# A four-layer graph network on one core: block transposes on VectorE with a scratch round trip in place of TensorE transposes, and rows spread by DMA

## The reference, cut to what matters

```
layer 0:  e = leaky((x W1)(x W2)^T), masked by adj, softmax over rows, times (x W3), relu
layer 1:  h = x W;  e[i,j] = leaky(s1[i] + s2[j]), masked, softmax, times h, elu
layer 2:  o1 = relu(x mlp1 + b1)
          h = o1 W_fc;  e[i,j] = leaky(f1[i] + f2[j]), no mask, softmax, times h, elu, elu, + o1
          o3 = relu(that mlp2 + b2)
          h = o3 W_hand; e[i,j] = leaky(f1[i] + f2[j]), masked, softmax, times h, elu, elu, + o3, relu
layer 3:  q, k, v; four heads of 64 channels; masked softmax of q k^T / 8, times v, times wo + bo
```

## Time and profile before

| | |
|---|---|
| median of 3 runs | 2921.91 us |
| the profiled execution | 2918.28 us |
| its span | 2916.5 us |
| mean granted TensorE clock | 0.983 of full speed |
| PE busy | 92% of the span |
| DVE, ACT, POOL busy | 78%, 69%, 53% |
| DMA queue q1, share of 16 engines | 22.7% |
| DMAs that SP issues for a graph | 13 |

### The profile page before, as it was taken

How to read it: one execution, slowest core, us unless ns; L and a number is a source line. 1 busy time by engine, 2 the same in 40 slices (tenths; PEclk the granted TensorE clock), 3 DMA queues, 4 the chain that set the end, 5 groups by cost and what they waited for, 6 DMA issues and landing times.

```text
span 2916.5 us, 61536 instructions
## 1 busy us (share of the span) xinstructions
PE 2689.4 (92%) x22472; PEld 2551.3 (87%) x22472; DVE 2278.2 (78%) x6124; ACT 1998.7 (69%) x4801; POOL 1556.0 (53%) x2119
## 2 busy tenths in 40 slices
PE   4689999999999999999999999999999999999974
PEld 4589999999999999998999998999999999998863
DVE  3257888888888888888888887888888888888874
ACT  1357777777777776777777777777777777776752
POOL 0235555555555555555556555555655555555542
PEclk9799999999999999999999999999999999999997
DMA  3001222222122122212212221221222122122222
GB/s 109 19 16 37 77 81 64 57 81 80 41 80 81 59 63 80 74 47 81 80 51 71 81 72 49 81 81 48 74 81 70 52 80 80 41 81 73 66 66 73
DMA packets 132766, 195.17 MB, mean 67 GB/s; under 512 B 14832, under 2 KB 97136, under 8 KB 132464
## 3 DMA queue, kind: packets, MB, share of 16 engines
q1 hardware_dynamic: 132464, 191.24, 22.7%
HBM read 107.30 MB, written 83.89 MB: 66 GB/s over the span
## 4 chain that ended last, share of the span: by engine, by line
PE 60%; DMA 13%; ACT 8%; SPq 8%; DVE 6%; issue 4%; POOL 1%; POOLq 0%; DVEq 0%
PE ps L224 29%; DMA p4T<-scratch 10%; PE ps L378 6%; SPq L208 6%; PE ps L240 5%; PE ps L436 4%; PE ps L337 4%; PE ps L233 3%; PE ps L338 3%; DMA scratch<-p 3%; DVE p L950 3%; PE ps L456 2%; ACT p L671 2%; PE ps L360 2%; DVE h_lo L692 1%
## 5 line engine op out<-in xcount | busy, mean ns | idle before, releaser
L1067 POOL TENSOR_TENSOR p<-p,rd 128x512 f32<-128x512 f32 x256 | 269.8, 1054 | 20.0
L671 ACT ACTIVATE p<-p,nmx 128x256 f32<-128x256 f32 x512 | 255.7, 504 | 25.4 <-DVE nmx L935 25.2
L991 POOL TENSOR_TENSOR o1Tp_lo<-o1T,o1Tp_hi 128x1024 fp32r<-128x1024 f32 x64 | 153.8, 2403 | 220.8 <-ACT o1Tp_hi L472 220.8
L1003 POOL TENSOR_SCALAR xn<-act,nmean,rstd 128x256 f32<-128x256 f32 x384 | 243.6, 643 | 18.3 <-POOL rstd L998 11.2
L456 PE MATMUL ps<-p4T,v 128*64 128x256 f32 x1024 | 144.3, 404 | 118.2 <-DMA p4T<-scratch 117.7
L995 POOL TENSOR_TENSOR vare<-mv,eps 128x2 f32<-128x2 f32 x256 | 108.0, 422 | 270.5 <-DVE mv L748 270.5
L1060 POOL TENSOR_TENSOR rd<-some,den 128x2 f32<-128x2 f32 x256 | 53.5, 209 | 354.6 <-DVE den L944 354.6
L456 PEld LDWEIGHTS ps<-p4T,v 128*64 128x64 f32 x1024 | 67.3, 140 | 178.1 <-DMA p4T<-scratch 96.5
L692 DVE TENSOR_TENSOR xnT_lo<-ps,xnT_hi 128x512 fp32r<-128x512 f32 x192 | 132.1, 688 | 114.2 <-ACT xnT_hi L472 114.2
L935 DVE CUSTOM_DVE_ANT_0 p<-ps,mask 128x256 f32<-128x256 f32 x512 | 189.9, 418 | 33.3 <-PE ps L436 33.3
L480 ACT ACTIVATE sco<-sco,nmax 128x256 f32<-128x256 f32 x384 | 191.0, 500 | 28.9 <-DVE nmax L736 28.9
(11 more groups left out here) (248 smaller groups left out, 12683.1 us busy)
## 6 DMA issues: line engine op xcount, KB each, us to landing
scratch<-p SPq DMA_DIRECT2D x128, 512.0 KB, 2.9
p4T<-scratch SPq DMA_DIRECT2D x512, 128.0 KB, 3.9
x0T<-in_xT SPq DMA_DIRECT2D x64, 256.0 KB, 4.6
x<-in_x SPq DMA_DIRECT2D x64, 256.0 KB, 3.7
out<-xn SPq DMA_DIRECT2D x64, 256.0 KB, 3.0
o1T<-in_mlp SPq DMA_DIRECT2D x1, 512.0 KB, 4.4
p<-in_mlp SPq DMA_DIRECT2D x1, 512.0 KB, 4.5
att<-in_fc SPq DMA_DIRECT2D x1, 512.0 KB, 5.4
```

The source lines that it names most:

```text
L671: ins = nc.scalar.activation(rows_, rows_, ACT.Exp, scale=-1.0, bias=nmx4[:, h, m:m + 1], accum_out=den4[:, h, m:m + 1])
L991: return G.tensor_tensor(lo, whole, hi.bitcast(fp32), ALU.subtract)
L1003: ins = G.tensor_scalar(xn[:, m, :], y[:, m, :], nmean[i][:, m:m + 1], rstd[i][:, m:m + 1], ALU.add, ALU.mult)
L1067: G.tensor_tensor(rows_, rows_, rd4[:, h, :].unsqueeze(2).unsqueeze(3).broadcast_to([P, NT, QUADS, CT * QP]), ALU.mult).then_inc(S["p4n"], 1)
```

## The change

All turning of probabilities follows the pattern of layer 3. `t0`, `t1`, `t3` on DVE turn 32 by 32 blocks of `sco` into the buffer `act`; SP writes `act` to scratch (`o0`, `o1`, `o3`) and reads it back into `sco` with four DMAs (`i0`, `i1`, `i3`); ACT copies the high part from there and POOL now makes the low part. The mixed layer's output takes the same way (`o3` on DVE through `sco[2]`, then `o5` and `i5` on SP into the new `o3r`), and `r3` adds it in two instructions. The spread of columns is done by SP: `r1`, `r2`, `r3` write 256, 512 and 256 single numbers from `cols` to scratch, `f1`, `f2`, `f3` read the row back into all 128 partitions. The sums of layer 2 are made by four matmuls of 256 columns against a full square of ones, and DVE takes the reciprocal of all 256 of them. `n4` moves to POOL. `xn3` and `sco` change in shape or number, `x0T` and `pfc` share the memory of their low parts, the banks of PSUM get other tenants, and all five tables are new.

```diff
-    "sp": "lt:0 o40:7 st:9 o42:7 lx:1 i40:7 i42:7",
-    "pe": "h3:8 a0:3 v4:9 f3:8 x0:5 g0:2 s40:9 d2:7 x1:6 t3:8 s42:9 v2:7 a3:8 m2:6 h0:2 b2:7 n2:6 o3:8 w2:7 s0:2 h1:5 c2:6 f1:5 t0:2 a4:9 r2:6 t1:5 x3:8 y4:9 m3:7 n3:7 a1:5 f2:6 q4:8 k4:8",
+    "sp": "r2:5 f2:5 st:9 o5:6 r3:6 o1:3 lx:1 f3:6 lt:0 i1:3 o3:6 o0:1 i3:6 i0:1 i5:6 o40:7 r1:2 o42:7 f1:2 i40:7 i42:7",
+    "pe": "k4:8 n2:5 d2:6 v4:8 v2:6 s40:8 w2:6 x0:3 s42:8 a1:4 h1:3 c2:5 a3:7 g0:1 r2:5 a0:2 m3:6 h0:1 x1:4 a4:8 h3:6 m2:4 s0:1 x3:7 y4:8 q4:7",
...
+            def pro_out(i):
+
+                def step(t):
+                    sp.wait_ge(S[f"pro{i}_x"], t + 1)
+                    wait(sp, S[f"pro{i}_dma"], back(t - 1))
+                    sp.dma_start(scratch_pro[i].rearrange("p w n -> p (w n)"), flat(act[i])).then_inc(S[f"pro{i}_dma"], 16)
+                return step
+
+            def pro_in(i):
+
+                def step(t):
+                    sp.wait_ge(S[f"pro{i}_dma"], sent(t))
+                    rows_ = sco[i][:, :, :, :].rearrange("p b a n -> p (b a n)").rearrange("p (q n) -> p q n", q=QUADS)
+                    for w in range(QUADS):
+                        sp.dma_start(rows_[w * QP:(w + 1) * QP, :, :], scratch_pro[i][:, w, :].rearrange("(q j) n -> j q n", q=QUADS)).then_inc(S[f"pro{i}_dma"], 16)
+                return step
...
+            def at_out(i):
+
+                def step(t):
+                    sp.wait_ge(S[f"at{i}"], t + 1)
+                    wait(sp, S[f"at{i}_dma"], back(t - 1, 1))
+                    sp.dma_start(scratch_at[i].rearrange("m p -> p m"), cols[i][:, :, 1], allow_slow_non_contiguous=True).then_inc(S[f"at{i}_dma"], 16)
+                return step
+
+            def at_in(i, tile, before):
+
+                def step(t):
+                    sp.wait_ge(S[f"at{i}_dma"], sent(t, 1))
+                    wait(sp, *before(t))
+                    sp.dma_start(tile[:, :, 0, :], scratch_at[i].unsqueeze(0).broadcast_to([P, NT, P])).then_inc(S[f"at{i}_dma"], 16)
+                return step
...
-            def t0(t):
-                pe.wait_ge(S["pro0"], t + 1)
-                transposes(bank[0], sco[0]).then_inc(S["proT0_mm"], 1)
...
-                for m in range(NT):
-                    for k in range(NT):
-                        for i in (1, 0):
-                            ins = nc.tensor.matmul(ps[:, 5, 2 * m:2 * m + 2], pfcp[i][:, k, m * P:(m + 1) * P], ones2[:, :],
-                                                   start=(k == 0 and i == 1), stop=(k == NT - 1 and i == 0))
+                for k in range(NT):
+                    for i in (1, 0):
+                        ins = nc.tensor.matmul(ps[:, 5, 0:N], ones2[:, :], pfcp[i][:, k, :], start=(k == 0 and i == 1), stop=(k == NT - 1 and i == 0))
...
             def u1(t):
-                ac.wait_ge(S["f1_mm"], t + 1)
-                graph_scores(1, 1).then_inc(S["raw1"], 1)
+                ac.wait_ge(S["at1_dma"], back(t, 1))
+                graph_scores(sco[1], 1).then_inc(S["raw1"], 1)
...
             def t0(t):
-                dv.wait_ge(S["proT0h"], t + 1)
-                low_part(proT[0], bank[0]).then_inc(S["proT0"], 1)
+                dv.wait_ge(S["pro0"], t + 1)
+                wait(dv, S["xn0"], t)
+                turn(0).then_inc(S["pro0_x"], 1)
...
             def d2(t):
                 dv.wait_ge(S["d2_mm"], t + 1)
-                V.reciprocal(rdc[:, :], ps[:, 5, 0:4:2]).then_inc(S["rdc"], 1)
+                wait(dv, S["att"], t)
+                V.reciprocal(rdb[:, :], ps[:, 5, 0:N]).then_inc(S["rdb"], 1)
...
             def r3(t):
-                dv.wait_ge(S["on3_mm"], t + 1)
+                dv.wait_ge(S["o3_dma"], back(t))
                 dv.wait_ge(S["q3"], t + 1)
-                V.tensor_tensor(act[2][:, :, :], act[2][:, :, :], bank[2], ALU.add).then_inc(S["r3"], 1)
+                for m in range(NT):
+                    row = act[2][:, m, :].rearrange("p (k q c) -> p k q c", k=CT, q=QUADS)
+                    ins = V.tensor_tensor(row, row, o3r[:, :, :, m, :].rearrange("p q k c -> p k q c"), ALU.add)
+                ins.then_inc(S["r3"], 1)
...
+            def n4(t):
+                norm(3, xn3, xn3, S["rstd3"], S["xn3"], t)
...
+            def t0(t):
+                po.wait_ge(S["proT0h"], t + 1)
+                low_of_turned(proT[0], 0).then_inc(S["proT0"], 1)
```

More of the change, by code:

```diff
@@ L163, in by_quads, with by_tiles, flat, sent @@
             return row.rearrange("p (b w j) -> p w b j", b=CT, w=QUADS)
+        def by_tiles(row):
+            return row.rearrange("p (b n) -> p b n", b=CT)
+        def flat(tile):
+            return tile[:, :, :].rearrange("p a n -> p (a n)")
+        def sent(t, n=QUADS):
+            return 16 * (n + 1) * t + 16
+        def back(t, n=QUADS):
+            return 16 * (n + 1) * (t + 1)
         def wait(eng, sem, n):
@@ new lines, in pro_in, with o3_out @@
+            def pro_in(i):
[5 more added lines that the diff above has]
+                return step
+            def o3_out(t):
+                sp.wait_ge(S["o3_x"], t + 1)
+                wait(sp, S["o3_dma"], back(t - 1))
+                sp.dma_start(scratch_o3.rearrange("p w n -> p (w n)"), sco[2][:, :, :, :].rearrange("p b a n -> p (b a n)")).then_inc(S["o3_dma"], 16)
@@ new lines, in o3_in @@
+            def o3_in(t):
+                sp.wait_ge(S["o3_dma"], sent(t))
+                wait(sp, S["r3"], t)
+                rows_ = o3r[:, :, :, :, :].rearrange("p q k a c -> p q (k a c)")
+                for w in range(QUADS):
+                    sp.dma_start(rows_[w * QP:(w + 1) * QP, :, :], scratch_o3[:, w, :].rearrange("(q j) n -> j q n", q=QUADS)).then_inc(S["o3_dma"], 16)
+            def at_out(i):
[4 more added lines that the diff above has]
+                return step
@@ L196, in turn_out, with at2_in @@
+            def at2_in(t):
+                sp.wait_ge(S["at2_dma"], sent(t, 2))
+                wait(sp, S["u"], t)
+                for c in range(2):
+                    sp.dma_start(by_tiles(row2[:, c, :]), scratch_at[2][c::2, :].unsqueeze(0).broadcast_to([P, NT, P])).then_inc(S["at2_dma"], 16)
             def turn_out(c):
@@ L198, in step @@
                     sp.wait_ge(S["p4x"], 2 * t + c + 1)
-                    wait(sp, p4Tin[c], 16 * QUADS * t)
-                    sp.dma_start(scratch[c], p4[c][:, :, :]).then_inc(p4out[c], 16)
+                    wait(sp, p4_dma[c], back(t - 1))
+                    sp.dma_start(scratch[c], p4[c][:, :, :]).then_inc(p4_dma[c], 16)
                 return step
@@ L240, in transposes @@
                         ins = nc.tensor.transpose(dst[:, b, a * P:(a + 1) * P], src[:, a, b * P:(b + 1) * P], ident[:, :])
-                return ins
-            def spread(dst, col):
-                for m in range(NT):
-                    ins = nc.tensor.transpose(dst[:, m * P:(m + 1) * P], col(m).broadcast_to([P, P]), ident[:, :])
                 return ins
@@ L375, in mlp2 @@
-            def mlp2(m):
-                for k in range(HT):
-                    for i, (a, b) in enumerate(PAIRS):
-                        ins = nc.tensor.matmul(bank[3][:, m, :], WP["mlp2"][a][:, k, m * P:(m + 1) * P], o2T[b][:, k, :],
-                                               start=(k == 0 and i == 0), stop=(k == HT - 1 and i == 2))
-                return ins
+                pe.wait_ge(S["pfcl"], t + 1)
+                enter(5, "att", t + 1)
+                product3(half_of(5), hfc, pfcp, NT, 2, off=2).then_inc(S["w2_mm"], 1)
@@ L395, in f3 @@
-            def f3(t):
-                pe.wait_ge(S["h3"], t + 1)
-                spread(ps[:, 3, 0:N], lambda m: cols[3][:, m, 1:2]).then_inc(S["f3_mm"], 1)
-            def t3(t):
-                pe.wait_ge(S["pro2"], t + 1)
-                transposes(bank[3], sco[2]).then_inc(S["proT2_mm"], 1)
+                enter(2, "h3", t + 1)
+                enter(3, "h3", t + 1)
+                product3(lambda m: ps[:, 2 + m, 0:C2], o3Tp, WP["hand"], CT, NT).then_inc(S["h3_mm"], 1)
             def a3(t):
@@ L735, in masked, with turn @@
                 for m in range(NT):
-                    ins = V.tensor_tensor_reduce(sco[i][:, m, :], whole(m), mask16[:, m, :], -1.0, BIG, ALU.add, ALU.min, nmax[i][:, m:m + 1])
+                    ins = V.tensor_tensor_reduce(sco[i][:, :, m, :], whole(m), by_tiles(mask16[:, m, :]), -1.0, BIG, ALU.add, ALU.min, nmax[i][:, m:m + 1])
                 return ins
+            def turn(i):
+                blocks = sco[i][:, :, :, :].rearrange("p b a n -> p (b a) n").rearrange("p c (w j) -> p w c j", w=QUADS)
+                return V.transpose(flat(act[i]).rearrange("p (w c j) -> p w c j", w=QUADS, j=QP), blocks)
             def stats(i, y, s_y, s_mv, t):
@@ L844, in v2 @@
                 dv.wait_ge(S["w2_mm"], t + 1)
+                dv.wait_ge(S["rdb"], t + 1)
                 wait(dv, S["o2T"], t)
```

370 lines of the change are left out of this document (209 added, 161 removed), and 6 rows, old and new, of the table ORDERS.

## The result

The changed kernel takes 4382.99 us (median of 4 runs, 4382.29 to 4389.12), the kernel before 2923.6 us on the same chip: a ratio of 1.500, 95% interval 1.497 to 1.503. The forecast was 2775 us and the range ended at 2920. It is half as slow again, far beyond even the slower rival's 3035.

A forecast was written before the change was run, and what follows sets the result against it. PE was taken to bound the kernel, busy 41.08 of each 42.64 us. PE's 37.4 plus 1.9 of chain and slower trips gave period 40.0; 52 x 40.0 plus 690 gave a 2770 span, 2775 us; range 2645 to 2920.

The forecast's parts named there:

- the slower rival: Trips r1 with f1 and r3 with f3 in SP's queue take 7.1 us each: period 45.0, 3035 us; chance 0.18.
- the second chain: From s42's end through layer 1's column trip to h3: 21.6 us, 1.9 beyond the 19.65 of PE's work there.
- the 3.9 of the nearest reads: Landing time assumed for layer 1's column write r1 and read f1; with issues, 8.66 us for the two.
- the latest landing of a load: 6.7 us, which with its issue gave 7.1 us a column trip, 2.5 more than the assumed 4.63.
- the prediction's own signs of being wrong: Landings under 3 or over 6 us, reciprocal over 1 us, no PE wait over 0.3, or PE waiting for DVE before s42.
- Hidden in sum: DMA work of 29 us in a period of 40, some 5000 packets added a graph, would not bound; bursts would meet.
- PE's work: PE's busy time a round falls from 41.08 to 37.4 us as transposes, spreads, narrow sums and some returns leave.
- DVE's work: DVE's busy time a round rises from 35.13 to 36.4 us through o3's turn, the wide reciprocal and blocked operands.
- The reciprocal of 256 columns: On DVE for layer 2, taken as 0.45 us, +0.3 over the narrow one, with +1.0 kept as the upper case.
- The penalty of 1.45 us for two operands in SBUF: DVE's b2, r3, e1, e3 lose their PSUM operand and contend with POOL: 0.36 us each, 1.45 together.
- the rival with DVE's order: DVE's order becomes the bound, 36.4 us of work plus 5.2 idle: period 41.6, 2860 us; chance 0.19.
- The forecast's own 40.0: Period: PE's 37.4 us plus 1.9 from the second chain, plus 0.3 for each of two trips under load.

The follow-up runs named there:

- By runs: Changed kernel with columns turned on DVE before going to scratch, written in pieces of 32 numbers (128 B) instead of single numbers: 2878.92 us, ratio 0.986 to before.
- the spread on PE: Changed kernel with the seven column DMAs removed and eight transposes on PE spreading the columns as before; scratch trips of probabilities stay: 2869.34 us, ratio 0.983.
- the last experiment: The mixed version with a3 and g0 exchanged in PE's order, so that a3 stands behind g0: 2801.7 us, ratio 0.961.
- the mixed version: Changed kernel with layer 2's column through scratch in 128 B pieces, those of layers 1 and 3 spread on PE: 2800.02 us, ratio 0.960 from three runs.

## Why the prediction was wrong

- **The step that failed** is the landing in the second chain: "for the landing I take the 3.9 of the nearest reads". For the reads back it was near (4.3 us for `f2`, 4.0 for `f3` in the round shown), but `r1` is a write of single numbers: 8.6 to 10.2 us from issue to landing for the three columns, and 8.7 in the median for such a write in the kernel before. The upper bound of the slower rival, "the latest landing of a load", was also a bound from another kind of DMA. The prediction said itself that no row shows a written transfer of 4 bytes; then the bound should have stayed open upwards, and the range with it. The slower rival named the right place, with a chance of 0.18; the range ended at 2920, below even that rival's 3035. Two of the prediction's own signs of being wrong came: landings over 6 us and a reciprocal over 1 us.
- **The waits were added up in the wrong place.** The second chain, and so the sum, held the way of one column, out by `r1` and back by `f1`; the slower rival named `r3` too, but added 2.5 us only twice. There are three columns, and SP's order makes a series of them: it waits for each write before it issues what stands behind. From the issue of a write to that of its read pass 8.6, 9.3 and 10.2 us in the round shown, 28.15 together. By runs it is 3.0, 2.5 and 1.6 (SP issues at 1497.06 and 1500.02, 1506.42 and 1508.92, 1513.79 and 1515.38), 7.05 together and 21.1 less. The period differs by 65.55 - 41.95 = 23.6 between the two forms. What makes the other 2.5 was not measured apart; PE's busy time, 44.63 us at a clock of 0.82 against 38.9 at 1.00, is the likely part.
- **Hidden in sum** was right for the load and useless for the time: 7110 packets a round, forecast as some 5000 more than before, and a DMA share of 0.40 (0.45 by runs). In the 6 us before the read of `r2` no engine moved anything. Bandwidth was not short there; completion was late.
- The Trainium skill, DMA: Bandwidth & Descriptors, section "Specifications", asks for transfers of at least 512 B, since smaller ones are read, modified and written. The runs agree with its direction (256 numbers of 4 B land after 8.7 us), but runs of 128 B, also under its bound, let their read go 2.5 us after the issue. No run here tests the reason that the page gives. I let the rule feed only the slower rival, at a price from loads.
- **PE's work** was put at 37.4 us. By runs it is 38.9 (1482.45 / 1600 x 41.95), and 38.85 with eight transposes back on PE. The direction held, 1.5 of the 3.7 did not come; PE's restarts after waits are in it, and how much they make was not settled.
- **DVE's work** was put at 36.4 and is 1990.13 / 54 = 36.85 after. That is luck, as two terms failed the opposite ways. The reciprocal of 256 columns takes 1.74 us, where 0.45 was taken and 1.16 was the upper bound:

```profile
L927 DVE RECIPROCAL rdb<-ps x64: 1720/1740/1757, 183.7 to 4268.8; 128x256 f32<-128x256 f32 x64
L922 DVE TENSOR_TENSOR pfcp<-pfcp,row x64: 691/693/695, 179.4 to 4252.4; 128x512 f32<-128x512 f32 x64
L1002 DVE SCALAR_TENSOR_TENSOR act<-act,xn x64: 654/676/693, 259.7 to 4332.8; 128x512 f32<-128x512 f32 x64
```

  It costs by the column: 1.74 / 256 = 6.8 ns each, against one turned element's 1.3 (0.67 / 512). The Trainium skill, VectorE: DVE Perf Modes, section "Walkthrough: the 8-slice pipeline in each mode", names it an iterative divide with a repeat count of 8; this trace agrees in kind, about five times a turn's price. The penalty of 1.45 us for two operands in SBUF came only in small part. The addition with the spread column in layer 2 (L922) takes 693 ns flat, as the form with PSUM had the earlier trace rows; `e1` and `e3` take 423 ns in the median for 128x256, where `e0`, still from PSUM, takes 418; only `r3` pays, 1.03 us on the average for its two in place of 0.69. The last line is the very operation of the earlier trace rows with the median of 1050: it takes 676 ns in the new order, with the same operands. So two SBUF operands alone don't make the penalty; what runs beside them is the likely cause, which was not tried. Other operations grew in turn: the three instructions `act<-act` from 1.82 to 2.53 us a graph.
- **What held only in looks.** By runs the period is 41.95, close to the 41.6 of the rival with DVE's order. But with the spread on PE the period was about the same (41.89), and there less work on DVE made it longer and a move in PE's order made it shorter: PE's order paced. Only the last experiment points to DVE, at 40.70. The forecast's own 40.0 lies near the mixed version's 40.66, which is another kernel; the mechanism behind 40.0 was not the one that ran.

## What to carry to other kernels

Give a DMA its price by its own kind and shape of piece; if no row shows one, say that the upper end is unknown, and turn the data so that pieces are runs (here 32 numbers, 128 B) before they leave. In one ordered queue, add up every write that is read back a place or two later, wherever the engines' chains lie. When a wait is taken away and the time stays, look at whose waits stayed the same: that engine is the one to suspect, and a run that takes work from it can settle it.

## What the hardware showed that I had not expected

- 256 numbers of 4 B written to DRAM: 8.7 us to landing, 32 numbers: 4.0, 512: 10.5, at a DMA share of 0.24 to 0.40 over the full stretch. In the last 6.26 us before `r2` was reported as landed, the DMA engines moved nothing. 512 numbers in sixteen runs of 128 B are read back 2.5 us after the issue of the write.
- A DMA issued behind such a write lands late too: 10.8 us for 512 KB of probabilities, where the same write ahead of it took 2.7.
- A vector operation with the same two SBUF operands took 1050 ns in the median in one order of the engines and 676 in another.
- PE's granted clock fell to 0.50 in the 9 us after a stretch in which it worked 1.68 of 7.12 us; over the whole changed kernel it is 0.81, over the version by runs 0.98.
